# The last stage of a fused state-space and expert kernel: the self term's product over 128 rows instead of 48

## The reference, cut to what matters

```
xp = x_ssm @ W_xproj.T ;  B = xp[..., 1:17] ;  C = xp[..., 17:33]
A  = -exp(A_log)                                  # 1024 x 16
dB = (1 - dA) / (A + 1e-8) * B_t                  # dA = exp(A * dt_t)
h  = clip(dA * h + dB * x_t, -10, 10)
y_t = sum_n C_t[n] * h[:, n] + D_param * x_t
x  = x + (y * silu(z)) @ W_out.T                  # end of layer 1
x  = x + shared(layernorm(x)) + wsum * expert(layernorm(x)) + bias
```

## Time and profile before

| what | us |
|---|---|
| median of three runs | 4503.36 |
| the profiled execution, its own time | 4499.18 |
| its span, first to last instruction | 4497.4 |
| PE busy in the span | 4214.5 (94%) |
| DVE busy | 3671.7 (82%) |
| ACT busy | 3169.2 (70%) |
| POOL busy | 3132.2 (70%) |

### The profile page before, as it was taken

The page is one execution under the profiler, slowest core; times in us unless marked ns, Lnnn a source line. Parts: engine busy times, 40 slices in busy tenths (PEclk is TensorE's granted clock), DMA queues, the critical chain, the costliest instruction groups (busy, mean ns, idle before and its releaser), DMA issues. The chain is left out here.

```text
span 4497.4 us, 48927 instructions
## 1 busy us (share of the span) xinstructions
PE 4214.5 (94%) x14186; PEld 2452.6 (55%) x14186; DVE 3671.7 (82%) x4320; ACT 3169.2 (70%) x5820; POOL 3132.2 (70%) x1548
## 2 busy tenths in 40 slices
PE   2999999995999999999999999999999479999999
PEld 1777777773444444444444444444444157777777
DVE  5888888884899999999999999999999634444443
ACT  1666666664999999999999999999999411111111
POOL 0111111110899999999999999999999567777772
PEclk9999999997999999999999999999999789999999
DMA  5666566666577557756665676567755445555550
GB/s 185 195 203 203 193 198 210 209 203 197 155 191 190 163 169 191 191 162 168 191 189 162 170 191 191 162 170 191 191 163 159 147 152 156 169 161 160 158 157 30
DMA packets 579687, 786.69 MB, mean 175 GB/s; under 512 B 101312, under 2 KB 304448, under 8 KB 577880
## 3 DMA queue, kind: packets, MB, share of 16 engines
q1 hardware_dynamic: 568856, 762.57, 57.8%
q10 hardware_dynamic: 10560, 20.97, 1.3%
HBM read 540.17 MB, written 245.18 MB: 175 GB/s over the span
## 5 line engine op out<-in xcount | busy, mean ns | idle before, releaser
L965 POOL TENSOR_TENSOR q<-g,cc 128x1024 f32<-128x1024 f32 x1024 | 2393.6, 2369 | 138.9 <-DVE g L1105 121.1
L1105 DVE TENSOR_TENSOR_SCAN g<-dd,carry,ps_a 128x512 f32<-128x512 f32 x2048 | 2400.0, 1255 | 37.5 <-ACT ps_a L987 24.4
L1045 PE MATMUL ps_y<-q,w_s 128*128 128x512 f32 x4096 | 2098.9, 593 | 20.0 <-POOL q L965 11.4
L987 ACT ACTIVATE ps_a<-dt_s,small 128x512 f32<-128x512 f32 x2048 | 1502.2, 734 | 5.4 <-DVE g L1105 5.4
L976 ACT ACTIVATE dd<-ps_d 128x512 f32<-128x512 f32 x2048 | 1287.9, 629 | 74.3 <-PE ps_d L1032 49.2
L1032 PE MATMUL ps_d<-dm,xk 99*128 99x512 f32 x2048 | 1103.6, 540 | 62.6 <-DMA dm<-band_d 25.5
L1032 PEld LDWEIGHTS ps_d<-dm,xk 99*128 99x128 f32 x2048 | 383.9, 188 | 1240.8 <-ACT dd L976 985.0
L1045 PEld LDWEIGHTS ps_y<-q,w_s 128*128 128x128 f32 x4096 | 777.2, 191 | 168.7 <-issue 49.7
L353 POOL TENSOR_TENSOR xnt_lo<-xnt_f,xnt_hi 128x512 fp32r<-128x512 f32 x64 | 110.3, 1723 | 562.4 <-ACT xnt_hi L378 562.4
L499 PE MATMUL ps_r_f<-xnt_hi,w_hi 128*128 128x512 f32 x1024 | 418.4, 409 | 13.8 <-DVE w_lo L672 13.8
L499 PE MATMUL ps_r_f<-xnt_lo,w_hi 128*128 128x512 f32 x1024 | 403.3, 394 | 0.0
(11 more groups left out here) (160 smaller groups left out, 4442.8 us busy)
## 6 DMA issues: line engine op xcount, KB each, us to landing
w_s<-w_d SPq DMA_DIRECT2D x256, 512.0 KB, 3.8
xk<-xt_d SPq DMA_DIRECT2D x768, 132.0 KB
xt_d<-xt_f SPq DMA_DIRECT2D x256, 256.0 KB, 3.0
cc<-c_d SPq DMA_DIRECT2D x128, 512.0 KB, 11.4
dm<-band_d SPq DMA_DIRECT2D x192, 264.0 KB
xs_d<-xs_f SPq DMA_DIRECT2D x128, 256.0 KB, 2.6
zs_d<-zs_f SPq DMA_DIRECT2D x128, 256.0 KB, 2.9
dt_d<-lg_f SPq DMA_DIRECT2D x32, 1024.0 KB, 6.8
```

The costliest lines, as they stand in the source:

```text
L965: pool.tensor_tensor(q[:, s % QB:s % QB + 2, :], g[:, s % GB:s % GB + 2, :], rows, ALU.mult).then_inc(s_q, 2)
L987: act.activation(ps_a[:, s % AB, :], dt[:, blk % DTB, :], ACT.Exp, scale=small[:, blk % MD, S_A + n:S_A + n + 1]).then_inc(s_a, 1)
L1045: pe.matmul(ps_y[:, blk % 2, :], w[:, half % WB, at:at + P], q[:, s % QB, :], start=(n == 0), stop=(n == NS - 1)).then_inc(s_n, 1)
L1105: dve.tensor_tensor_scan(g[:, s % GB, :], dd[:, m % 2, n, :], ps_a[:, s % AB, :], carry[:, m, n:n + 1], ALU.add, ALU.mult).then_inc(s_g, 1)
```

## The change

The three groups of 16 rows move to partitions 0, 32 and 64, so that the rows in use end at 80 (`ROWS3`). The two operands of the product, `inv_c` and `b_r`, become 128 rows high, and the product runs over all 128; the rows between and behind the groups hold zeros in both. To have these zeros, POOL fills `c_r` and all of `x_c[:, 1]` with zeros and copies `c_r` to `b_r` before anything is loaded there, and SP waits for that. The table is now staged in `x_c[:, 1]`, in two halves of columns, with six loads for three; ACT and DVE treat it in two instructions each. `load_rows` has six transfers for two. POOL's work per chunk is over rows 0 to 79 for 0 to 47.

```diff
-    ROWS3 = 3 * NS
+    GROUP, ROWS3 = 32, 2 * 32 + NS
...
-        inv = sb("inv_c", [ROWS3, MD, P], F32R, c)
+        inv = sb("inv_c", [P, MD, P], F32R, c)
...
-        b_r, c_r = sb("b_r", [ROWS3, CH], F32R, c), sb("c_r", [ROWS3, CH], c=c)
+        b_r, c_r = sb("b_r", [P, CH], F32R, c), sb("c_r", [P, CH], c=c)
...
-        raw_inv = t_lo[0:ROWS3, 0:2, :, :].rearrange("p k s t -> p (k s) t").bitcast(F32)
+        raw_inv = [x[:, 1, :, (2 + h) * P:(3 + h) * P] for h in range(2)]
...
-                        for dst, r0 in ((b_r[:, :].bitcast(F32), 1), (c_r[:, :], 1 + NS)):
+                        for dst, r0 in ((b_r, 1), (c_r, 1 + NS)):
                             src = xp_d[ch // NCH, r0:r0 + NS, bass.ds(ch % NCH * CH + 1, CH)]
-                            sp.dma_start(dst, bass.AP(tensor=src.tensor, offset=src.offset,
-                                                      ap=[(0, 3), (PAD, NS), (1, CH)])).then_inc(s_rows, 16)
+                            for r in range(3):
+                                at = dst[GROUP * r:GROUP * r + NS, :]
+                                sp.dma_start(at.bitcast(F32) if dst is b_r else at, src).then_inc(s_rows, 16)
...
+                sp.wait_ge(s_set, 3)
                 for r in range(3):
-                    sp.dma_start(raw_inv[NS * r:NS * (r + 1), :, :], w_d[:, 0:NS, W_INVT:W_INVT + P]
-                                 .rearrange("m n p -> n m p")).then_inc(s_wt[0], 16)
+                    for h in range(2):
+                        sp.dma_start(raw_inv[h][GROUP * r:GROUP * r + NS, :, :], w_d[h::2, 0:NS, W_INVT:W_INVT + P].rearrange("m n p -> n m p")).then_inc(s_wt[0], 16)
...
-                        pool.wait_ge(s_rows, 32 * ch + 32)
-                        pool.tensor_tensor(c_r[:, :], b_r[:, :].bitcast(F32), c_r[:, :], ALU.mult).then_inc(s_pr, 1)
+                        pool.wait_ge(s_rows, 96 * ch + 96)
+                        pool.tensor_tensor(c_r[0:ROWS3, :], b_r[0:ROWS3, :].bitcast(F32), c_r[0:ROWS3, :], ALU.mult).then_inc(s_pr, 1)
...
+                pool.memset(c_r[:, :], 0.0).then_inc(s_set, 1)
+                pool.memset(x[:, 1, :, :], 0.0).then_inc(s_set, 1)
+                pool.wait_ge(s_set, 1)
+                pool.tensor_copy(b_r[:, :], c_r[:, :]).then_inc(s_set, 1)
                 pool.memset(gate[:, :, :], -1.0).then_inc(s_set, 1)
-                pool.memset(raw_g, 0.0).then_inc(s_set, 1)
...
+                def upper_inverse():
+
+                    act.wait_ge(s_wt[0], 96)
+                    for h in range(2):
+                        last = act.activation(inv[:, h::2, :], raw_inv[h], ACT.Copy)
+                    last.then_inc(s_hi, 1)
...
-                    at_lo = slice(2 * NS, ROWS3)
-                    dve.tensor_tensor(inv[at_lo, :, :], raw_inv[at_lo, :, :], inv[at_lo, :, :].bitcast(F32), ALU.subtract)\
-                        .then_inc(s_lo, 1)
+                    at_lo = slice(2 * GROUP, ROWS3)
+                    for h in range(2):
+                        last = dve.tensor_tensor(inv[at_lo, h::2, :], raw_inv[h][at_lo, :, :], inv[at_lo, h::2, :].bitcast(F32),
+                                                 ALU.subtract)
+                    last.then_inc(s_lo, 1)
```

More of the change, by code:

```diff
@@ L1182, in ffn @@
         YL = MD // 2
-        raw_inv = t_lo[0:ROWS3, 0:2, :, :].rearrange("p k s t -> p (k s) t").bitcast(F32)
+        raw_inv = [x[:, 1, :, (2 + h) * P:(3 + h) * P] for h in range(2)]
         raw_g = x[:, 1, :, 0:P]
-        parts = ((raw_inv, inv[:, :, :], None),
+        parts = ((None, None, None),
                  (o[:, 0, :, :], wo_hi[:, 0:HALF, :], wo_lo[:, 0:HALF, :]),
@@ L1266, in _ @@
                 load_x(0)
-                sp.wait_ge(s_set, 2)
+                sp.wait_ge(s_set, 4)
                 sp.dma_start(raw_g[:, :, 0:GATES], t_in["W_gate"].rearrange("(k p) n -> p k n", p=P)).then_inc(s_wt[5], 16)
@@ L1295, in weigh_rows @@
                     if ch < CHUNKS:
-                        pool.wait_ge(s_rows, 32 * ch + 32)
-                        pool.tensor_tensor(c_r[:, :], b_r[:, :].bitcast(F32), c_r[:, :], ALU.mult).then_inc(s_pr, 1)
+                        pool.wait_ge(s_rows, 96 * ch + 96)
+                        pool.tensor_tensor(c_r[0:ROWS3, :], b_r[0:ROWS3, :].bitcast(F32), c_r[0:ROWS3, :], ALU.mult).then_inc(s_pr, 1)
                         pool.wait_ge(s_pr, 2 * ch + 1)
-                        pool.tensor_copy(b_r[:, :], c_r[:, :]).then_inc(s_pr, 1)
+                        pool.tensor_copy(b_r[0:ROWS3, :], c_r[0:ROWS3, :]).then_inc(s_pr, 1)
                         pool.wait_ge(s_pr, 2 * ch + 2)
@@ L1353, in upper_weights @@
                 def upper_weights(i):
-                    act.wait_ge(s_wt[i], 48 if i == 0 else 16)
+                    act.wait_ge(s_wt[i], 16)
                     act.activation(parts[i][1], parts[i][0], ACT.Copy).then_inc(s_hi, 1)
+                def upper_inverse():
[3 more added lines that the diff above has]
+                    last.then_inc(s_hi, 1)
                 def upper_y(ch):
@@ L1381, in _ @@
                 load_weights(4, "W_expertT", 0)
-                for i in range(3):
+                upper_inverse()
+                for i in range(1, 3):
                     upper_weights(i)
```

## The result

| | before | after |
|---|---|---|
| median of the runs, us | 4500.85 (4 runs) | 4454.41 (4453.17 to 4456.56, 4 runs) |
| the profiled execution, us | 4499.18 | 4454.84 |
| its span, us | 4497.4 | 4453.1 |

The change makes the kernel faster by 1.1%: the ratio is 0.9894, with a 95% interval of 0.9883 to 0.9906. The median before is 4500.85 us here, over one run more than was shown ahead of the prediction. Forecast was 4463.7 us, 39.7 less; measured are 46.4 less between medians and 44.3 between the two profiled executions.

The account below looks back on a forecast made before the run. PE's stream was taken to bound the loop. Loop -41.1, ahead of the loop -0.6 and start +2 made -39.7 us, from 4503.36 to 4463.7 us, range 4453 to 4476.

Parts of the forecast that it names:

- What bounds the kernel: Loop over chunks: PE alone bounds each 54.00 us pass, so what its stream saves is saved until another engine is late.
- The price of a self-term product: Loop: eight cost 4.80 us a pass, 0.60 each; at 0.233 each a pass takes 51.07, 41.1 us less over 14 passes.
- That height is what matters: Loop: going from 128 rows to 48 and back breaks the shadowed weight loading; 99 rows beside 128 showed no break.
- The rule that loading weights takes as long for few rows as for many: Skill rule leading to the rival that height doesn't matter: the loop gains nothing, the start is paid, 4509 us; chance 3 in 100.
- Who could be late next: Loop: POOL's remainder of y is the latest delivery, with 7.7 us slack, so nothing of the 2.93 us is given back.
- Ahead of the loop: First two chunks: three self-term products of chunk 1 save 0 to 1.1 us, taken as 0.6; chunk 0's save nothing.
- The start of the stage: Last stage's start: SP waits for POOL and issues more transfers; y's load is issued 5.7 us later, costing 2 us.
- three parts of the 5.7: Start of the stage: SP starts 3.2 us later, six table loads add 1.3, six transfers of rows add 1.2.
- the working's two ends: Start of the stage: delay nothing, or a gain bounded at 2 us, if DMA engines stay full; otherwise all, 7.6 at most.
- the 3558 to 3565: Start of the stage: sign that DVE's first self term should run at 3558 to 3565 us.
- The sum: Whole kernel: -41.1 - 0.6 + 2 = -39.7 us, from 4503.36 to 4463.7 us.
- the widening for the medians: Whole kernel: the terms' 4458.6 to 4469.9 us widened at both ends by about 6, to 4453 to 4476.

Follow-up runs that it names:

- the second pair of profiles: The kernel before and the changed kernel, each run once more without an edit: 4500.92 and 4455.97 us.
- the plain fp32 products: Changed kernel with the four 8-row gate transposes turned into plain products over 128 rows with zeros below row 8: 4466.03 us, ratio 0.9918.

## Why the prediction was right

**What bounds the kernel.** Right. PE's stream in the loop is the time of the loop, before and after, to 0.01 us a pass.

**The price of a self-term product.** Right: 4.80 us for eight by the comparison with the pass without them. After, the eight have 51.04 - 49.20 = 1.84 us, 0.230 each, between the 0.2275 and the 0.233 that were its ends. The 13 later passes have won 38.4 us, 2.95 each for the 2.93 forecast, which makes 41.3 for 14 passes against 41.1. The first pass won 3.3, and 0.4 of that isn't height: its first 12 products stand ahead of any self term and take 4.78 us before and 4.38 after. PE comes out of a wait there at the lower clock, its products 0.43 us apart, and in the changed kernel the clock rose two products sooner. In the second pair of profiles the first pass won 4.3 us.

**That height is what matters.** Right, and now shown and not only argued: 48 and 64 rows 54.00 us, 65 rows 51.08, 128 rows 51.04, at the same start and layout. The prediction had a gap between 48 and 99 rows in which the step had to lie. The Trainium skill, TensorEngine Tiling (Array Packing), sections Available Configurations and Key Properties, has a rule that would explain it: there are configurations of 32, 64 and 128 rows, and a change of mode drains the engine. The step between 64 and 65 rows agrees with that. No view shows the mode of a product or a drain, so that this is the cause stays argued. The rule that loading weights takes as long for few rows as for many, which the prediction weighed, holds for the instruction: 182 to 183 ns for 48 rows and 188 for 128. As the cost of the product in its place it is wrong here by 0.37 us. The gain isn't in a shorter instruction but in a load that may start while the former product runs.

The Trainium skill, TensorE: Matmul & The Clock Gate, section The mechanism, says in its list of what overlaps that loads overlap matmuls in flight only where their row groups differ; ahead of the list it also allows it to a load into a background weight buffer. With the list the trace disagrees: in the changed kernel the load of 128 rows at 3933.97 starts after the 128-row product at 3933.96 and before the one at 3934.20, and in the kernel before it was just the load of another height that didn't overlap. No view shows which buffer a load goes to.

**Who could be late next.** Right, nobody. POOL's remainder of y in the changed kernel:

```profile
3943.50 9.45 POOL L1324 TENSOR_TENSOR y_lo<-y_c,y_hi 128x1024 fp32r<-128x1024 f32 x4 [2.62 <-ACT y_hi L1375]
```

It ends at 3952.95, and the reader comes behind the transposes that start at 3959.17: a slack of 7.1 us for 7.7.

**Ahead of the loop.** Right: 0.6 us was forecast, and 0.6 is what the height gives there. The stretch has three steps of one kind, cut from one of DVE's additions to `x_c` to the next, each with one self-term product of chunk 1 behind a wait for DVE. The windows of one such step before, and of two in the changed kernel (columns as in the earlier trace rows):

```profile
3604.20:3614.20 10.00, 8.20 (x27) 5.90 (x27) 2.78 (x4) 0.00 (x0) 5.08 (x4) 0.83 0.58 187
3603.71:3613.52 9.81, 7.81 (x27) 5.96 (x26) 2.79 (x5) 0.00 (x0) 5.07 (x4) 0.83 0.52 160
3613.52:3621.77 8.25, 6.33 (x27) 4.81 (x26) 2.78 (x4) 0.00 (x0) 5.13 (x4) 1.00 0.32 90
```

The first two have the same clock, 0.83, and differ by 0.19 us: PE is idle ahead of the product, so a break there costs nothing, and behind it the two distances are 0.43 and 0.33 us before, 0.33 and 0.24 after. That is half of the 0.37 of the loop. Three make 0.6, and the upper end of 1.1 was out of reach. The third line isn't height. There the granted clock stayed at 1.00, and the step is 1.55 us shorter for it. In the eight profiles with 48, 64 or 32 rows 2 steps of 24 are short in this way (8.45 us for 9.96 to 10.00), in the six with more than 64 rows 5 of 18 (8.25 to 8.27 for 9.79 to 9.81). From the end of chunk 0's `y_lo` to the loop the eight have 57.6 to 58.7 us (mean 58.2) and the six 56.3 to 57.5 (mean 56.9). Of this 1.2 us half is height and half is the clock. Whether the change itself makes the clock stay up more often, so few profiles can't tell.

**The start of the stage.** Here a term was wrong, in size and in sign: +2 us was taken, within -2 to +7.6, and it was -1.0. This is the step that failed: six plain transfers for two threefold ones, taken as an added cost, were a gain. The working had the fill of 2048 columns at 2.1 us (1.80), SP's first load at 3.2 us later (2.9) and y's issue at 5.7 us later (4.6). The three parts of the 5.7 came nearly as priced, 2.9 + 1.6 + 1.2; but issuing the loads of D, xs and zs, which the working took as unchanged, went down from 4.4 us to 3.3. Of the later start all but about 0.5 us is hidden, as the kernel with SP later alone showed; that is near one of the working's two ends. What the working had not seen is that the old threefold transfers were dear: it priced the six new ones by their issue alone, as a pure addition, though the old ones stood at 0.77 us against 0.42 in the same rows and were the odd ones there. So the first self term of DVE runs at 3556.85, ahead of the 3558 to 3565 that the prediction gave as its sign.

**The sum.** Height in 14 passes -41.3, height ahead of the loop -0.6, the start -1.0. The clock adds about -1.5: one short step (1.55) less a first step that is 0.4 longer, and the 0.4 of the first pass. Together -44.4, and the stage begins 0.1 later: the 44.3 of the two profiled executions, for a forecast of -39.7. The mechanism and the size of the loop's gain were right; 3.0 us of the difference is the start's term. The 1.5 of the clock, for which the prediction had no term, is luck as far as these profiles tell. The remaining 2 us between 44.3 and the 46.4 of the medians are as much as the medians move with the stages that the change doesn't touch. The measured 4454.41 lies under the 4458.6 to which the terms alone reached, and is in the range by the widening for the medians; 2.5 us of that is that the median before went from 4503.36 to 4500.85 with its fourth run.

**A version that beats both?** The full-height gate transposes take 1.3 us off the changed kernel in the profile. In the runs (0.9897 with an interval of 0.0036) this isn't told apart from the changed kernel.

## What to carry to other kernels

In a stream of products on TensorE, look for the ones over at most 64 rows between neighbours over 128: a product over 48 rows there cost 0.37 to 0.39 us more than its fair 0.23, and padding it to over 64 rows with zeros gave that back at no cost in the loop. Where PE waits ahead of such a product, expect only half, here 0.19. Read it in the distances from start to start and in whether the weight load starts ahead of its product, not in the length of the instruction. Price it with a pass of the same trace that lacks the product, and before padding anything else check that the padded form doesn't turn into a dearer instruction, as the plain fp32 products did.

## What the runs showed of the hardware that was not expected

- The step in height lies exactly between 64 rows (54.00 us a pass) and 65 (51.08).
- A transfer that reads 16 rows of 2 KB three times by a stride of zero is worse than three plain ones: with two of them in front, the load of y landed 23.8 and 23.9 us after the stage's beginning, with six plain ones in their place 21.8 us, though issued 0.7 us later, and a 4-KB load behind them on the queue took 12.1 us and 6.6. No view shows how a transfer is spread over the 16 DMA engines, so the runs leave the cause open.
- A matmul on fp32 operands is two matmuls in the trace where a transpose is one: four took 0.81 us with 8 columns each.

The Trainium skill, DMA: Bandwidth & Descriptors, section Rules for kernel authors, has a rule that would explain the second point: a leading broadcast dimension of c copies confines the whole transfer to at most c engines. The old transfers had such a dimension of 3, the new ones lead with 16 rows. The direction of the measured 2 us agrees with it; that three engines were the ones in use isn't shown by any run here.
